# Attention laps: the query softmax's last product moved to POOL, and new orders on PE, DVE and POOL

## The chip, the cores and the metric

The kernel runs on one core of one Trainium2 chip. The metric is the device time of one execution in microseconds. TensorE is called PE here (its weight loads PEld), VectorE DVE, ScalarE ACT, GpSimd POOL, SyncE SP.

## The reference

One model layer over 8 rows of 512 tokens. The token part is a small recurrent memory, a layer norm, four feed-forward blocks of width 128 and 512, and a head to 64 values. Then comes linear attention with 4 heads of 32, and then a mixture of 8 experts with the best 2 per token. Each part is added to its own input. The change touches only the attention:

```python
xn = rmsnorm(x, g_pre)
q, k, v = split(xn @ w_qkv)              # 4 heads of 32, 4 memory columns are put before k and v
q = softmax(q, over the 32 of a head) * SCALE
k = softmax(k, over the sequence)
context = einsum('bhdn,bhen->bhde', k, v)
out = einsum('bhde,bhdn->bhen', context, q)
out = rmsnorm(out @ w_out + b_out, g_out) + x
```

## The kernel before

Everything stays in SBUF, and every engine has its own instruction list, written out by hand. Engines meet only at counting semaphores: `wait_ge(sem, n)` holds an engine's whole list until the count is reached. There are three stages: the token part (32 steps of a row and a layer, to about 248 us), the attention in nine overlapping laps (to about 318 us), and the experts (64 units of a row and an expert).

The laps are the loops `for m in range(FIRST_LAP, 0)`, one on each engine. This text counts them by a = m + 9, so lap 0 to lap 8. In lap a an engine works on several rows at once, each at another step: row a (keys, query projections), c = a - 1 (softmaxes, context), d = a - 2 (attend), e = a - 3 (output norm, residual), f = a - 4 (normalised input of the experts), and rows a + 1 to a + 3 (normalised input of the attention). k is the row's parity and picks one of two buffers.

The operations of a lap before the change, in order, with the lines of their instructions:

- PE: `k_transposes(c)` (L1675, L1676), `q_transposes(d)` (L1692, waits for `qn_ready`), `z_transposes(a+1)`, `context(c)`, `keep_clock` (three products whose result nobody reads), `projected_context(c)` (waits for `ctm_ready`), `expert_z_transposes(f)` (waits for `ezlo_ready`), `attend(d)` (waits for `m_ready`, for `qt_ready` and for `h1_ready` of row e), in lap 1 `head(7)`, `keys(a+1)` (waits for ACT's `zt_ready` and for `m_ready` of row c, whose bank it writes), `queries_and_values(a+1)`. Lap 7 has `logits(0)` at its end. Products recorded on L1430 are of several kinds, told apart by their tiles.
- DVE: `max_k(a)` (L1164), `negated` (L1168), `output_sums(e)` (L1216), `max_q(a)` (L1176), `sub_q(a)` (L1180), `softmaxes(c)` (L1190 to L1198), `z_of(a+2)` (L1092), `masked_context(c)` (L1205, waits for `ctx_done`), `expert_z_lo(f)` (L1235), `head_out` of row 5 or 6 in laps 0 and 1 (L1103), `scaled_output(e)` (L1224, waits for POOL's `r2_ready`), `z_lo(a+2)` (L1098), `scaled_m(c)` (L1210, waits for `m_done`), `residual_moments(e)` (L1074, L1077), in lap 1 `head_out(7)`, and in laps 0 to 2 `head_moments(a+5)`.
- ACT: `output_squares(e)`, `k_turned(c)`, `q_turned(d)`, `ez_of(f)` (L796, waits for POOL's `s1_ready`), `ez_hi(f)` (L802), `exp_k(a)`, `z_hi(a+2)` (L718), `z_turned(a+1)` (L756), `copy_v(a)`, `expert_z_turned(f)`, `exp_q(a)`.
- POOL: `expert_norm(f)` (L564 to L569), `centred(a+3)` (L540), `output_norm(e)` (L556, L558), `roots_of(a+3)` (L530, L531, L534), `residual_base(a+2)` (L548, L551, waits for DVE's `z_ready`). The powers in L534, L558 and L567 are inverse square roots.

PSUM has eight banks. The bank of `keys(a+1)` is the one that `context`, `projected_context` and `scaled_m` of row c use, so keys wait for `scaled_m(c)`.

Of the kernel before, what the change touches and what calls it, by code (L numbers as in the profile page):

```python
# [29 lines left out]
ALU = mybir.AluOpType  # L30
# [3 lines left out]
P = 128  # L34
B, S, V = 8, 512, 64
NT = S // P
# [3 lines left out]
HEADS, DH, NMEM = 4, 32, 4  # L40
# [112 lines left out]
def build(nc, tok_in, emb_in, wupd_in, wf_in, w1_in, w2_in, headw_in, cols_in, rows_in, cons_in,  # L153
          wqkv_in, wout_in, memv_in, wr_in, ew1_in, ew2_in, eb2_in, out_hbm):
    ctx = ExitStack()
    with ctx:
# [3 lines left out]
        def sem(name):  # L160
            return ctx.enter_context(nc.semaphore(name))
# [100 lines left out]
        q_sb = x  # L262
# [7 lines left out]
        qsum = sb("qsum", [P, 2, NT * HEADS])  # L270
        qrec = sb("qrec", [P, 2, NT * HEADS])
# [82 lines left out]
        k_done, qv_done = sem("k_done"), sem("qv_done")  # L354
        kmax_ready, kexp_ready, v_ready = sem("kmax_ready"), sem("kexp_ready"), sem("v_ready")
        qsub_ready, qexp_ready, qn_ready = sem("qsub_ready"), sem("qexp_ready"), sem("qn_ready")
        k_t, kt_ready, q_t, qt_ready = sem("k_t"), sem("kt_ready"), sem("q_t"), sem("qt_ready")
        ctx_done, ctm_ready, m_done, m_ready = (sem("ctx_done"), sem("ctm_ready"), sem("m_done"),
                                                sem("m_ready"))
# [23 lines left out]
        def row64(first):  # L383

            return rows[:, first:first + D2].unsqueeze(1).broadcast_to([P, NT, D2])

        def o_view(b):

# [60 lines left out]
        def _(pool):  # L449
# [93 lines left out]
            def residual_base(b):  # L543
# [6 lines left out]
                own.wait(v)  # L550
                pool.tensor_tensor(h0[:, b, :], h0[:, b, :], xc[:, b % 2, :], ALU.add).then_inc(res_ready, 1)  # L551

            def output_norm(b, k):

                pool.wait_ge(osum_ready, b + 1)
                v = own.inc(pool.tensor_scalar(e2o[:, k, :], osum[:, k, :], 1.0 / D2, 1e-24 / D2, ALU.mult, ALU.max))  # L556
                own.wait(v)
                pool.tensor_tensor(r2[:, k, :], e2o[:, k, :], mhalf[:, 0:NT], ALU.pow).then_inc(r2_ready, 1)  # L558

            def expert_norm(b, k):  # L560

                pool.wait_ge(mv1_ready, b + 1)
                mv, vi = mv1[:, k, :, :], h1v[:, k, :, :]
                v = own.inc(pool.tensor_scalar(vi[:, 0, :], mv[:, :, 1], 1.0 + EPS, EPS * EPS, ALU.mult, ALU.add))  # L564
                own.inc(pool.tensor_scalar(vi[:, 1, :], mv[:, :, 0], -1.0, None, ALU.mult))
                own.wait(v)
                v = own.inc(pool.tensor_tensor(s1[:, k, :], vi[:, 0, :], mhalf[:, 0:NT], ALU.pow))  # L567
                own.wait(v)
                pool.tensor_tensor(s1_shift[:, k, :], vi[:, 1, :], s1[:, k, :], ALU.mult).then_inc(s1_ready, 1)  # L569
# [4 lines left out]
                if b:  # L574
                    residual_base(b - 1)
            for m in range(FIRST_LAP, 0):
                a, e, f = m + 9, m + 6, m + 5
                if f >= 0:
                    expert_norm(f, f % 2)
                if a + 3 < B:  # L580
                    centred(a + 3)
                if e >= 0:
                    output_norm(e, e % 2)
                if a + 3 < B:
                    roots_of(a + 3)
                if a + 2 < B:
                    residual_base(a + 2)
# [306 lines left out]
        def _(dve):  # L894
# [206 lines left out]
            def head_out(b):  # L1101
                dve.wait_ge(head_done, b + 1)
                dve.tensor_tensor(tiles(h0[:, b, :]), tiles(bank[HEAD_BANK[b % 2]][:, 0:NT * D2]), row64(R_HEADB),  # L1103
                                  ALU.add).then_inc(h0_ready, 1)
# [76 lines left out]
                                  qmax[:, k, :].rearrange("p (t h) -> p t h", h=HEADS).unsqueeze(3)  # L1181
                                  .broadcast_to([P, NT, HEADS, DH]), ALU.subtract).then_inc(qsub_ready, 1)

            def q_by_head(b):
                return q_sb[:, b, :].rearrange("p (a d) -> p a d", d=DH)

            def softmaxes(b, k):

                dve.wait_ge(qexp_ready, b + 1)
                v = own.inc(dve.reduce_sum(qsum[:, k, :], q_by_head(b), AX.X))  # L1190
                v_k = own.inc(dve.tensor_scalar(kstat[:, k, 4:5], kstat[:, k, 2:3], kstat[:, k, 3:4], float(DH) ** 0.5,
                                                ALU.add, ALU.mult))
                own.wait(v)
                v = own.inc(dve.reciprocal(qrec[:, k, :], qsum[:, k, :]))
                own.wait(v_k)
                v_k = own.inc(dve.reciprocal(kstat[:, k, 5:6], kstat[:, k, 4:5]))
                own.wait(v)
                dve.tensor_tensor(q_by_head(b), q_by_head(b), qrec[:, k, :].unsqueeze(2)  # L1198
                                  .broadcast_to([P, NT * HEADS, DH]), ALU.mult).then_inc(qn_ready, 1)
                return v_k  # L1200

            def masked_context(b, k):

                dve.wait_ge(ctx_done, b + 1)
                dve.tensor_tensor(ctm[:, k, :], bank[4 * k + 1][:, P:2 * P], blkmask, ALU.mult).then_inc(ctm_ready, 1)  # L1205

            def scaled_m(b, k, v):
                own.wait(v)
                dve.wait_ge(m_done, b + 1)
                dve.scalar_tensor_tensor(mx_sb[:, b % 4, :], bank[4 * k + 1][:, 2 * P:3 * P], kstat[:, k, 5:6],  # L1210
                                         bout_share[:, :], ALU.mult, ALU.add).then_inc(m_ready, 1)
# [107 lines left out]
            for m in range(FIRST_LAP, 0):  # L1319
                a, c, e, f = m + 9, m + 8, m + 6, m + 5  # L1320
                if a < B:
                    max_k(a, a % 2)
                    negated(a % 2, own.n)
                if e >= 0:
                    output_sums(e, e % 2)
                if a < B:
                    max_q(a, a % 2)
                    sub_q(a, a % 2, own.n)
                if m == -1:
                    v = first_hot(0, v)  # L1330
                if c >= 0:
                    v_total[c] = softmaxes(c, c % 2)
                if a + 2 < B:
                    z_of(a + 2, a % 2)
                if c >= 0:
                    masked_context(c, c % 2)
                if f >= 0:
                    expert_z_lo(f, f % 2)
                if a == 0:
                    head_out(5)  # L1340
                if a == 1:
                    head_out(6)
                if e >= 0:
                    scaled_output(e, e % 2)
                if a + 2 < B:
                    z_lo(a + 2, a % 2)
                if m == -1:
                    v = second_max(0, v)
                if c >= 0:
                    scaled_m(c, c % 2, v_total[c])  # L1350
                if m == -1:
                    v = second_hot(0, v)
                if e >= 0:
                    residual_moments(e, e % 2)
                if m == -2:
                    take_logits(0)
                if m == -1:
                    v = weights(0, v)
                    gates_out(0, v)
                if m == -2:  # L1360
                    v = first_max(0)
                if a == 1:
                    head_out(7)
                if a < 3:
                    head_moments(a + 5)
# [62 lines left out]
        def _(pe):  # L1428
# [335 lines left out]
            for m in range(FIRST_LAP, 0):  # L1764
                a, c, d, f = m + 9, m + 8, m + 7, m + 5
                if c >= 0:
                    k_transposes(c, c % 2)
                if d == 0:
                    pe.wait_ge(h0_ready, B)
                if d >= 0:  # L1770
                    q_transposes(d, d % 2)
                if a + 1 < B:
                    z_transposes(a + 1, (a + 1) % 2)
                if c >= 0:
                    context(c, c % 2)
                keep_clock(c)
                if c >= 0:
                    projected_context(c, c % 2)
                if f >= 0:
                    expert_z_transposes(f, f % 2)  # L1780
                if d >= 0:
                    attend(d, d % 2)
                if m == -1:
                    keep_clock(c)
                if a == 1:
                    head(7)
                if a + 1 < B:
                    keys(a + 1, (a + 1) % 2)
                if a == 0:
                    head(5)  # L1790
                if m == -1:
                    pe.wait_ge(late_weights, 4)
                    pe.wait_ge(m_ready, B)
                    hidden(0)
                    hidden(1)
                    turn_gates(0)
                if a + 1 < B:
                    queries_and_values(a + 1, (a + 1) % 2)
                if m == -2:
                    logits(0)  # L1800
                if a == 0:
                    head(6)
# [132 lines left out]
```

## Time and profile before

| what | value |
|---|---|
| median of 3 runs | 423.93 us (423.75 to 424.1) |
| the profiled execution | 424.18 us |
| its span in the trace | 422.4 us |
| mean granted clock of PE | 0.982 |
| instructions | 6309 |

The span is the time from the first to the last instruction; 1.8 us lie around it. The page tells each engine's busy time and the chain of work that ended last. The timelines give every instruction's start and duration; where several instructions of a line stand together, the row gives their number. Durations overlap a little: the next operation of an engine can start before the one in front of it is recorded as ended, so the step from start to start is what an operation costs its engine. What stands in square brackets is the idle time in front of the operation and who ended it.

### The profile page before, as it was taken

How to read it: one execution, taken by the hardware profiler on the slowest of the kernel's cores; microseconds unless marked ns; L12 is line 12 of the kernel's file. 1: busy time of each engine (PE TensorE's matmuls, PEld its weight loads, DVE VectorE, ACT ScalarE, POOL GpSimd, SP SyncE). 2: the span in 40 equal slices, each digit the busy share in tenths (PEclk: the TensorE clock that was granted, in tenths of full speed). 3: DMA queues.
4: the chain of work that ended last, by engine and by line, in shares of the span. 5: the costliest groups of instructions: out<-in, count | busy, mean ns of one | idle time of the engine just before them, and what ended most of it. 6: DMA issues, size and time to landing. Idle time of an engine off the chain costs nothing.

```text
span 422.4 us, 6309 instructions
## 1 busy us (share of the span) xinstructions
PE 394.1 (93%) x1989; PEld 318.0 (75%) x1989; DVE 352.6 (83%) x851; ACT 326.1 (77%) x558; POOL 262.2 (62%) x388
## 2 busy tenths in 40 slices
PE   5798889999999999999999989999987998999995
PEld 2586578888888888888888878787766775876883
DVE  4887688888898889888889888999875888899885
ACT  1263689999999999888977854678846898988994
POOL 0575787778777779778776556685322654435452
PEclk9999999999999999999999998999996998999999
DMA  6800012122312321221112000000000000000001
GB/s 217 334 2 0 2 26 46 31 51 51 50 27 50 51 53 27 50 50 50 44 32 51 1 0 2 2 2 2 0 2 0 0 2 12 15 12 12 14 13 26
DMA packets 15849, 14.94 MB, mean 35 GB/s; under 512 B 9796, under 2 KB 10568, under 8 KB 15560
## 3 DMA queue, kind: packets, MB, share of 16 engines
q1 hardware_dynamic: 15816, 14.54, 13.8%
q8 instruction: 16, 0.26, 0.2%
q14 instruction: 17, 0.14, 0.1%
HBM read 13.42 MB, written 1.11 MB: 34 GB/s over the span
## 4 chain that ended last, share of the span: by engine, by line
PE 64%; DVE 18%; ACT 12%; issue 4%; DMA 1%; POOL 1%; SPq 0%; DVEq 0%; ACTq 0%
PE ps L1430 56%; PE ps L1453 4%; ACT hid L861 4%; ACT w_all L867 3%; ACT ezf L796 2%; DVE hid L1372 2%; DVE hh L1224 2%; DVE stats L941 1%; DVE x L1372 1%; PE ps L1461 1%; DVE st L1074 1%; DVE kstat L1164 1%; DMA xn<-in_w_f 1%; DVE xn_lo L1379 1%; DVE qmax L1176 1%
## 5 line engine op out<-in xcount | busy, mean ns | idle before, releaser
L675 ACT ACTIVATE hid<-ps,b_fold 128x512 f32<-128x512 f32 x128 | 84.0, 681 | 21.3 <-PE ps L1430 20.8
L1015 DVE TENSOR_TENSOR hid_lo<-hid,hid_hi 128x1024 fp32r<-128x1024 f32 x64 | 78.8, 1231 | 25.3 <-ACT hid_hi L680 25.1
L1430 PE MATMUL ps<-xn_hi,w_all 128*128 128x512 f32 x256 | 87.4, 402 | 0.6 <-DVE xn_lo L1010 0.6
L1430 PE MATMUL ps<-hid_hi,w_all 128*128 128x512 f32 x256 | 85.0, 393 | 0.0
L680 ACT ACTIVATE hid_hi<-hid 128x1024 fp32r<-128x1024 f32 x64 | 67.9, 1061 | 2.0
L1430 PEld LDWEIGHTS ps<-xn_hi,w_all 128*128 128x128 f32 x256 | 48.4, 189 | 10.8 <-issue 0.9
L1430 PEld LDWEIGHTS ps<-hid_hi,w_all 128*128 128x128 f32 x256 | 48.1, 188 | 9.9
L1430 PE MATMUL ps<-xn_lo,w_all 128*128 128x512 f32 x128 | 49.9, 390 | 0.0
L1430 PE MATMUL ps<-hid_lo,w_all 128*128 128x512 f32 x128 | 49.8, 389 | 0.0
L861 ACT ACTIVATE hid<-ps,eb_fold 128x512 f32<-128x512 f32 x64 | 44.1, 689 | 1.4 <-PE ps L1430 1.2
L1430 PE MATMUL ps<-hid_hi,ew 128*128 128x512 f32 x128 | 43.1, 421 | 1.9 <-ACT hid L861 1.8
L1372 DVE TENSOR_TENSOR hid<-hid,ps 128x512 f32<-128x512 f32 x44 | 30.0, 683 | 11.2 <-ACT hid L861 7.7
L941 DVE BATCH_NORM_STATS2 stats<-ps 128x6 f32<-128x128 f32 x160 | 35.2, 282 | 2.8 <-PE ps L1453 2.8
L490 POOL TENSOR_TENSOR var_in<-var_in 128x4 f32<-128x4 f32 x30 | 35.7, 1191 | 2.4
L486 POOL TENSOR_TENSOR var_in<-stats 128x4 f32<-128x4 f32 x30 | 17.6, 586 | 25.6 <-DVE stats L941 25.6
L1430 PE MATMUL ps<-w_all,ew 128*128 128x512 f32 x84 | 31.6, 415 | 1.2 <-DVE xn_lo L1379 0.7
L494 POOL TENSOR_TENSOR var_in<-var_in,mhalf 128x4 f32<-128x4 f32 x30 | 31.1, 1036 | 2.3
L1453 PEld LDWEIGHTS ps<-cons,x 128*128 128x128 f32 x160 | 23.2, 187 | 10.9 <-issue 5.3
L867 ACT ACTIVATE w_all<-hid 128x512 fp32r<-128x512 f32 x44 | 28.0, 636 | 4.3 <-DVE hid L1372 4.2
L1430 PEld LDWEIGHTS ps<-hid_hi,ew 128*128 128x128 f32 x128 | 23.8, 197 | 9.4 <-ACT hid L861 4.8
L1453 PE MATMUL ps<-cons,x 128*128 128x128 f32 x160 | 25.5, 281 | 5.3 <-DVE stats L941 2.9
L1430 PE MATMUL ps<-hid_lo,sel 128*128 128x512 f32 x64 | 27.2, 424 | 1.8 <-ACT hid_lo L817 0.8
(222 smaller groups left out, 898.2 us busy)
## 6 DMA issues: line engine op xcount, KB each, us to landing
rstd_row<-roots SPq DMA_DIRECT2D x29, 256.0 KB, 3.8
hh<-in_tokens SPq DMA_DIRECT2D x8, 256.0 KB, 7.9
hid<-in_w SPq DMA_DIRECT2D x1, 1024.0 KB, 7.1
rstd_row<-in_w SPq DMA_DIRECT2D x1, 1024.0 KB, 10.2
out<-hh SPq DMA_DIRECT2D x7, 128.0 KB, 2.0
ew_raw<-in_expert_w SPq DMA_DIRECT2D x1, 512.0 KB, 9.7
roots<-rstd SPq DMA_DIRECT2D x29, 2.0 KB, 1.4
ew_raw<-in_expert_w SPq DMA_DIRECT2D x1, 256.0 KB, 9.9
```

Source lines behind the costliest of these rows:

```text
L486: own.inc(pool.tensor_tensor(vi[:, 0, :], st[:, :, 1], st[:, :, 4], ALU.subtract))
L490: own.inc(pool.tensor_tensor(vi[:, 0, :], vi[:, 0, :], vi[:, 0, :], ALU.mult))
L494: v = own.inc(pool.tensor_tensor(vi[:, 0, :], vi[:, 2, :], mhalf[:, 0:NT], ALU.pow))
L675: act.activation(hid[:, j % 2, f, :], bank[f], ACT.Gelu, bias=b1_fold[:, j // B * F + f:j // B * F + f + 1]).then_inc(gelu_done, 1)
L680: act.activation(hid_hi[:, j % 2, 2 * p:2 * p + 2, :], hid[:, j % 2, 2 * p:2 * p + 2, :], ACT.Copy).then_inc(hhi_ready, 1)
L861: act.activation(hg[:, n % NHG, :], bank[HIDDEN_BANK[n % 2]], ACT.Gelu, bias=eb1_fold[:, n % E:n % E + 1]).then_inc(eg_done, 1)
L867: act.activation(hw_hi[:, slot * S:(slot + 1) * S], hw(slot), ACT.Copy).then_inc(hwhi_act, 1)
L941: last = dve.bn_stats(stats6[:, slot, t, :], bank[TB][:, t * P:(t + 1) * P])
L1015: dve.tensor_tensor(hid_lo[:, j % 2, 2 * p:2 * p + 2, :], hid[:, j % 2, 2 * p:2 * p + 2, :], hid_hi[:, j % 2, 2 * p:2 * p + 2, :].bitcast( ...
L1372: dve.tensor_tensor(hw(slot), hg[:, n % NHG, :], bank[spread_bank(n)], ALU.mult).then_inc(hw_ready, 1)
L1430: return pe.matmul(out, lhsT, rhs, start=start, stop=stop)
L1453: last = pe.transpose(bank[TB][:, t * P:(t + 1) * P], part, ident)
```

## The change

Four edits in the laps:

1. DVE's product of q's exponentials with the reciprocals of their sums (L1198) goes. POOL does it in a new `softmax_of_queries(c)`, which waits for the new semaphore `qrec_ready`.
2. POOL's lap becomes `expert_norm(f)`, `output_norm(e)`, `softmax_of_queries(c)`, `centred(a+3)`, `roots_of(a+3)`, `residual_base(a+2)`.
3. On DVE `masked_context(c)` comes before `z_of(a+2)`, and `scaled_m(c)` before `scaled_output(e)`.
4. On PE `keys(a+1)` comes before `attend(d)`, and so in lap 1 before `head(7)`.

```diff
--- before.py
+++ after.py
@@ -354,6 +354,7 @@
         k_done, qv_done = sem("k_done"), sem("qv_done")
         kmax_ready, kexp_ready, v_ready = sem("kmax_ready"), sem("kexp_ready"), sem("v_ready")
         qsub_ready, qexp_ready, qn_ready = sem("qsub_ready"), sem("qexp_ready"), sem("qn_ready")
+        qrec_ready = sem("qrec_ready")
         k_t, kt_ready, q_t, qt_ready = sem("k_t"), sem("kt_ready"), sem("q_t"), sem("qt_ready")
         ctx_done, ctm_ready, m_done, m_ready = (sem("ctx_done"), sem("ctm_ready"), sem("m_done"),
                                                 sem("m_ready"))
@@ -383,6 +384,9 @@
         def row64(first):
 
             return rows[:, first:first + D2].unsqueeze(1).broadcast_to([P, NT, D2])
+
+        def q_by_head(b):
+            return q_sb[:, b, :].rearrange("p (a d) -> p a d", d=DH)
 
         def o_view(b):
 
@@ -550,6 +554,12 @@
                 own.wait(v)
                 pool.tensor_tensor(h0[:, b, :], h0[:, b, :], xc[:, b % 2, :], ALU.add).then_inc(res_ready, 1)
 
+            def softmax_of_queries(b, k):
+
+                pool.wait_ge(qrec_ready, b + 1)
+                pool.tensor_tensor(q_by_head(b), q_by_head(b), qrec[:, k, :].unsqueeze(2)
+                                   .broadcast_to([P, NT * HEADS, DH]), ALU.mult).then_inc(qn_ready, 1)
+
             def output_norm(b, k):
 
                 pool.wait_ge(osum_ready, b + 1)
@@ -574,14 +584,15 @@
                 if b:
                     residual_base(b - 1)
             for m in range(FIRST_LAP, 0):
-                a, e, f = m + 9, m + 6, m + 5
+                a, c, e, f = m + 9, m + 8, m + 6, m + 5
                 if f >= 0:
                     expert_norm(f, f % 2)
+                if e >= 0:
+                    output_norm(e, e % 2)
+                if c >= 0:
+                    softmax_of_queries(c, c % 2)
                 if a + 3 < B:
                     centred(a + 3)
-                if e >= 0:
-                    output_norm(e, e % 2)
-                if a + 3 < B:
                     roots_of(a + 3)
                 if a + 2 < B:
                     residual_base(a + 2)
@@ -1181,9 +1192,6 @@
                                   qmax[:, k, :].rearrange("p (t h) -> p t h", h=HEADS).unsqueeze(3)
                                   .broadcast_to([P, NT, HEADS, DH]), ALU.subtract).then_inc(qsub_ready, 1)
 
-            def q_by_head(b):
-                return q_sb[:, b, :].rearrange("p (a d) -> p a d", d=DH)
-
             def softmaxes(b, k):
 
                 dve.wait_ge(qexp_ready, b + 1)
@@ -1191,13 +1199,9 @@
                 v_k = own.inc(dve.tensor_scalar(kstat[:, k, 4:5], kstat[:, k, 2:3], kstat[:, k, 3:4], float(DH) ** 0.5,
                                                 ALU.add, ALU.mult))
                 own.wait(v)
-                v = own.inc(dve.reciprocal(qrec[:, k, :], qsum[:, k, :]))
+                dve.reciprocal(qrec[:, k, :], qsum[:, k, :]).then_inc(qrec_ready, 1)
                 own.wait(v_k)
-                v_k = own.inc(dve.reciprocal(kstat[:, k, 5:6], kstat[:, k, 4:5]))
-                own.wait(v)
-                dve.tensor_tensor(q_by_head(b), q_by_head(b), qrec[:, k, :].unsqueeze(2)
-                                  .broadcast_to([P, NT * HEADS, DH]), ALU.mult).then_inc(qn_ready, 1)
-                return v_k
+                return own.inc(dve.reciprocal(kstat[:, k, 5:6], kstat[:, k, 4:5]))
 
             def masked_context(b, k):
 
@@ -1330,24 +1334,24 @@
                     v = first_hot(0, v)
                 if c >= 0:
                     v_total[c] = softmaxes(c, c % 2)
+                if c >= 0:
+                    masked_context(c, c % 2)
                 if a + 2 < B:
                     z_of(a + 2, a % 2)
-                if c >= 0:
-                    masked_context(c, c % 2)
                 if f >= 0:
                     expert_z_lo(f, f % 2)
                 if a == 0:
                     head_out(5)
                 if a == 1:
                     head_out(6)
+                if c >= 0:
+                    scaled_m(c, c % 2, v_total[c])
                 if e >= 0:
                     scaled_output(e, e % 2)
                 if a + 2 < B:
                     z_lo(a + 2, a % 2)
                 if m == -1:
                     v = second_max(0, v)
-                if c >= 0:
-                    scaled_m(c, c % 2, v_total[c])
                 if m == -1:
                     v = second_hot(0, v)
                 if e >= 0:
@@ -1778,14 +1782,14 @@
                     projected_context(c, c % 2)
                 if f >= 0:
                     expert_z_transposes(f, f % 2)
+                if a + 1 < B:
+                    keys(a + 1, (a + 1) % 2)
                 if d >= 0:
                     attend(d, d % 2)
                 if m == -1:
                     keep_clock(c)
                 if a == 1:
                     head(7)
-                if a + 1 < B:
-                    keys(a + 1, (a + 1) % 2)
                 if a == 0:
                     head(5)
                 if m == -1:
```

## Rows read from the trace of the kernel before

**Rows 1.** The page's first part: each engine's busy time, share of the span and instructions.
```profile
PE 394.1 (93%) x1989; PEld 318.0 (75%) x1989; DVE 352.6 (83%) x851; ACT 326.1 (77%) x558; POOL 262.2 (62%) x388
```

**Rows 2.** The chain that ended last, in order of time, lap 5: start, us, what.
```profile
289.45 2.67 PE ps L1430 x18
```

**Rows 3.** The timeline of PE in lap 1: start us, us, what, count.
```profile
259.66 0.38 PE L1430 MATMUL ps<-wout,scratch 128*128 128x128 f32 x2
259.88 1.00 PE L1430 MATMUL ps<-headw,x 128*128 128x64 f32 x8
```

**Rows 4.** The timeline of DVE, laps 1 to 6, the same columns.
```profile
260.92 0.42 DVE L1103 TENSOR_TENSOR hh<-ps,rows 128x256 f32<-128x256 f32 x1 [0.38 <-PE ps L1430]
...
265.05 0.25 DVE L1194 RECIPROCAL qrec<-qsum 128x16 f32<-128x16 f32 x1
...
272.69 0.42 DVE L1092 TENSOR_TENSOR scratch<-scratch,sr 128x256 f32<-128x256 f32 x1
...
286.97 0.69 DVE L1198 TENSOR_TENSOR x<-x,qrec 128x512 f32<-128x512 f32 x1
...
289.24 0.85 DVE L1098 TENSOR_TENSOR w_all<-scratch,w_all 128x256 fp32r<-128x256 f32 x1
...
296.07 0.85 DVE L1224 SCALAR_TENSOR_TENSOR hh<-ps,r,hh 128x64 f32<-128x64 f32 x4
```

**Rows 5.** The timeline of POOL, laps 2 to 5.
```profile
266.53 0.61 POOL L548 TENSOR_TENSOR scratch<-scratch,sr 128x256 f32<-128x256 f32 x1 [4.26 <-DVE scratch L1092]
...
268.09 0.62 POOL L540 TENSOR_TENSOR scratch<-hh,mv 128x256 f32<-128x256 f32 x1
269.93 0.26 POOL L556 TENSOR_SCALAR e2o<-osum 128x4 f32<-128x4 f32 x1 [1.22 <-DVE osum L1216]
...
271.28 0.23 POOL L530 TENSOR_SCALAR sr_in<-mv 128x4 f32<-128x4 f32 x1
...
271.75 1.67 POOL L534 TENSOR_TENSOR sr<-sr_in,mhalf 128x8 f32<-128x8 f32 x1
...
283.94 0.19 POOL L564 TENSOR_SCALAR h1v<-mv 128x4 f32<-128x4 f32 x1
...
285.81 0.23 POOL L556 TENSOR_SCALAR e2o<-osum 128x4 f32<-128x4 f32 x1
...
289.08 0.72 POOL L551 TENSOR_TENSOR hh<-hh,scratch 128x256 f32<-128x256 f32 x1
```

**Rows 6.** POOL's groups by shape: count, then busy us and mean ns of one.
```profile
L593 POOL TENSOR_TENSOR xn_lo<-hid,w_all 128x512 fp32r<-128x512 f32 x10 | 13.0, 1296 | 15.7 <-ACT w_all L867 15.7
```

**Rows 7.** The timeline of ACT in lap 5.
```profile
286.08 1.42 ACT L796 ACTIVATE ezf<-hh,s_shift,s 128x64 f32<-128x64 f32 x4
...
289.10 0.58 ACT L756 ACTIVATE xn_hi<-ps 128x512 fp32r<-128x512 f32 x1
```

**Rows 8.** The timeline of PE, laps 5 to 7.
```profile
297.07 1.13 PE L1430 MATMUL ps<-mx_sb,qT 128*128 128x128 f32 x8 [0.21 <-DVE hh L1224]
297.95 0.70 PE L1430 MATMUL ps<-xn_hi,wqkv 128*128 128x512 f32 x2
298.50 1.08 PE L1430 MATMUL ps<-wqkv,xn_hi 128*128 128x256 f32 x8
299.41 0.60 PE L1675 MATMUL ps<-cons,scratch 128*128 128x128 f32 x4
...
303.26 0.38 PE L1430 MATMUL ps<-wout,scratch 128*128 128x128 f32 x2
...
304.53 1.13 PE L1430 MATMUL ps<-mx_sb,qT 128*128 128x128 f32 x8 [0.21 <-DVE hh L1224]
```

**Rows 9.** PE in two-microsecond windows: stretch, us, busy, granted clock, DMA.
```profile
254.00:256.00 2.00, 2.00 (x11) 0.50 0.03 8
```

**Rows 10.** The timeline of PE where that clock was low.
```profile
252.70 1.18 PE L1430 MATMUL ps<-wqkv,xn_hi 128*128 128x256 f32 x8 [1.51 <-ACT rstd_row L773]
...
255.24 1.06 PE L1675 MATMUL ps<-cons,scratch 128*128 128x128 f32 x4
```

## The prediction

> **What bounds the kernel now.** The page's first part comes first: PE is busy 93% of the span, DVE 83%, ACT 77%, POOL 62% [rows 1]. That is an average, and the change touches only the nine attention laps (about 249 to 318 us), so the rest was read from the timelines of those laps, engine by engine, and from the chain in order of time. In the laps PE and DVE are both nearly full. DVE goes from the maximum of the keys to `scaled_output`, that lets `attend` start on PE, `attend` with the next keys and projections holds PE for 2.67 us in the chain [rows 2], and the keys let DVE begin its next lap. From lap 4 on the chain also runs through ACT's `ez_of`. One attend to the next takes 7.46 us in lap 6 (297.07 to 304.53) and 7.62 in lap 5 (289.45 to 297.07) [rows 2, 8]. POOL looks idle for a third of the time, but its order matters: each of its waits is a place where it is ahead. I write op(b) for an operation on row b, and all times of "after" below are worked out by walking the four engine queues from lap 1, each operation starting at the later of its engine and its waits.
>
> **The change part by part.**
>
> *The multiply leaves DVE.* Per row one 0.69 us operation goes at 286.97 [rows 4], about 0.61 from start to start. This is a gain on DVE only where DVE doesn't wait. After the change `masked_context` comes directly behind the reciprocals and needs the context from PE, whose loop doesn't get shorter, so most of the 0.61 turns into a wait there. I count it as nothing in the sum; its full worth stands in the first rival.
>
> *The multiply comes to POOL.* The nearest row is POOL's 128x512 product of the expert stage, 1.30 us [rows 6]; two of its 128x256 operations would be 1.22 (0.61 each) [rows 5]. I take 1.29. What is queued behind it counts more than its length: it waits for the reciprocals of its row, in the middle of DVE's lap, and `centred`, `roots_of` and `residual_base` of the lap, which used to run ahead, stand behind that wait. The pieces, start to start [rows 5]: output norm 1.35 (269.93 to 271.28), roots 2.14 (271.28 to 271.75 plus 1.67), residual 1.56 (266.53 to 268.09), centred 0.62, expert norm 1.87 (283.94 to 285.81). Lap 2 then asks 1.29+0.62+2.14+1.56 = 5.6 us of POOL, lap 3 with the output norm 7.0, lap 4 with the expert norm too 8.8, which is more than a lap is long. Together 21.4 us, without a wait in between.
>
> *The shared way to SBUF.* DVE's `z_lo` reads two SBUF tensors. While POOL's addition ran (289.08, 0.72) it took 0.85 us (289.24) [rows 4, 5], though such an operation takes 0.42 when undisturbed at 272.69 [rows 4]. POOL's multiply will meet `z_of` or `expert_z_lo` in every lap; the one that waited goes first when it ends, and then holds up `centred` by some 0.3. Three laps of this and one more for the roots: 1.2 us on POOL's queue. The low end is 0, if they never meet.
>
> The Trainium skill ("SBUF — State Buffer", Who interferes with whom) says that a Vector instruction with two SBUF inputs and a GpSimd instruction that reads SBUF exclude each other for the whole instruction. For streaming operations this trace agrees (0.85 against 0.42). For the power it does not: `z_of` at 272.69 took its plain 0.42 while POOL's 1.67 us power was running [rows 4, 5]. By the rule taken word for word every power would shut DVE out as well, before and after alike; by the rows only the new multiply does. It changes no term above.
>
> *Keys before attend on PE, and head 7 behind the keys (lap 1).* Keys(2) need `scaled_m(0)`, which needs the product that PE starts at 259.66 [rows 3]: 0.42 to its end, 0.49 for `scaled_m` (0.34 and the hand-over, an estimate by the 0.42 us rows), so keys(2) start about 260.6, hardly earlier than before. Head 7 used to fill this gap at 259.88 [rows 3]; now it starts after the 0.55 us keys (297.95 to 298.50 in lap 6) [rows 8], at 261.15, which is 1.27 later. DVE's `head_out(7)` (260.92 before) [rows 4] and all that follows it, so the whole of lap 2, come 1.27 later.
>
> *What that makes of POOL.* The reciprocals of row 1 come at 265.05 [rows 4] + 1.27, and 0.30 later, at 266.6, POOL starts its multiply. It then has work without a pause: 266.6 + 21.4 + 1.2 = 289.2 for the start of expert norm(1), which ran at 283.94 [rows 5]. So POOL, not DVE, sets laps 4 and 5. s1(1) follows 1.87 later at 291.1; ACT's `ez_of(1)` ran at 286.08 [rows 7].
>
> *What hangs on it.* ACT reaches the copy of z(6) 3.02 us behind that (286.08 to 289.10) [rows 7], at 294.1, and 0.6 on the keys(6) can start, 294.7. Here the new PE order costs: attend(3) stands behind these keys and starts 0.55 later, at 295.3, against 289.45 [rows 2]. From attend to the transposes of the next lap it was 2.34 (297.07 to 299.41) [rows 8] with the keys in it, 1.79 without. So they come at 297.1 instead of 289.45 + 2.5 (a small wait included) = 292.0. **Plus 5.1 us at the start of lap 6.**
>
> *Laps 6 to 8.* POOL has caught up. Now `scaled_m` lies between the projected context and `scaled_output`, so the loop is: attend 0.88, projections 0.91, transposes to projected context 3.85 (299.41 to 303.26), 0.42, `scaled_m` 0.27, `scaled_output` to attend 1.00 (296.07 to 297.07) [rows 4, 8] = 7.33, against 7.46. In lap 6 POOL's multiply holds `expert_z_lo` for 0.3, so it is 0.2 longer; in lap 7 there are no keys to take out of the loop, and only `scaled_m` 0.27 comes in: 0.3. Lap 8 waits for the expert rows before and after and gives nothing back, although DVE is 0.6 less loaded. Together 0.5.
>
> *The clock.* With POOL late, PE stands 1.8 to 2.2 us in front of the keys in laps 2, 4 and 5. After the 1.51 us idle before 252.70 the granted clock fell to 0.50 (1.2 GHz) in the stretch 254 to 256, and four transposes took 1.06 us instead of 0.60; waits of 0.2 us did nothing [rows 8 to 10]. In laps 2 and 4 a fall is hidden, because POOL sets what comes next. In lap 6 it is not: projections and transposes there would be some 0.8 longer. Between 0 and 1.3 I take 0.8, as our wait is nearer to the 1.51.
>
> **The sum:** 5.1 + 0.5 + 0.8 = 6.4 us. The expert stage behind it is unchanged and starts with the gates that lap 8 makes, so it moves as a whole. The profiled execution took 424.18 (its span 422.4 and 1.8 around it): 430.6. The median of the runs, 423.93, is 0.25 below that execution, so 430.3.
>
> **The rivals.**
> 1. *The cover holds* (faster). POOL's own idle time takes the multiply, and the keys never wait for ACT's copy. Then DVE has 0.61 less, and PE's own work is the floor: lap 6's 7.46 less the 0.21 idle before its attend [rows 8], 7.25. Three laps of 7.6 (lap 5 is one of them) and lap 6 come down to that: 3 x 0.37 + 0.21 = 1.3 us saved, 422.6. It decides at the place where expert norm(1) starts: at 284 or earlier it holds. Against it speaks the sum of POOL's lap 4, 8.8 us. 7%.
> 2. *POOL hardly binds, the orders do.* If the multiply costs POOL next to nothing, head 7's 1.27 and the keys ahead of attend still remain, since z(6) comes from ACT 0.6 before the keys: by the same walk 2.7 us, 426.6. For it: spans on POOL are rough. 14%.
> 3. *No collisions and no lower clock.* 5.1 + 0.5 - 1.3 = 4.3: 428.2. This is the low part of the forecast's own case.
> 4. *The clock falls in more laps, or the multiply with its broadcast operand takes 1.5 us.* 0.2 more in each of six multiplies is 1.2, and a second exposed fall 0.8: 432.3. 13%.
> 5. *Nothing changes*, DVE's gain and POOL's delay balancing: 3%.
>
> **How the numbers follow.** The forecast with its low part (3.) has 63%: 427.8 to 431.6. To leave out no more than 2 in 10 the range reaches down to the second rival and up through the fourth: 426.3 to 433.0. About 0.2% is what a measurement of this kernel can tell from no change: faster 0.07, within it 0.03, slower 0.90.
>
> **What would show it.** In the profile after: POOL without a pause from about 266.6 to 295, its multiplies 1.3 us each; expert norm(1) near 289 (at 284 the main term is wrong); `head_out(7)` near 262.2 (at 260.9 the first step is wrong); `z_of` or `expert_z_lo` of 0.8 to 1.4 us instead of 0.42; PE idle about 2 us before keys(5) and keys(6), with ACT's copy of z as releaser; attends at about 269.7, 277.2, 286, 295.3; a granted clock of 0.50 somewhere in laps 2 to 6 or none; laps 6 and 7 a little longer than before. If POOL is idle within laps 3 and 4, or DVE waits for nothing, the walk is wrong from its start.

## The result: 1.4% slower

The changed kernel takes 429.35 us, the median of 4 runs (427.87 to 429.83); the kernel before took 424.01 beside it. The ratio is 1.0136, with a 95% interval of 1.0109 to 1.0163, so about 5.3 to 5.8 us more. The profiled execution is the fastest of the four: 427.87, with a span of 426.1.

The first part of the page after, to be read against [rows 1]:

```profile
PE 391.4 (92%) x1989; PEld 314.9 (74%) x1989; DVE 349.3 (82%) x843; ACT 326.5 (77%) x558; POOL 270.2 (63%) x396
```

POOL is busy 8 us more (eight multiplies of 1.05), DVE 3.3 less. The averages say nothing of a loss; the order of the work does. The lines of the changed kernel are shifted by some: its multiply is L560, expert norm L574 to L579, roots L538, `z_of` L1103, `expert_z_lo` L1239, `masked_context` L1209, `head_out` L1114. The timeline of POOL in laps 2 to 5, as [rows 5] of before:

```profile
265.59 1.05 POOL L560 TENSOR_TENSOR x<-x,qrec 128x512 f32<-128x512 f32 x1 [3.66 <-DVE qrec L1202]
...
272.88 1.05 POOL L560 TENSOR_TENSOR x<-x,qrec 128x512 f32<-128x512 f32 x1 [0.42 <-DVE qrec L1202]
...
278.26 0.19 POOL L574 TENSOR_SCALAR h1v<-mv 128x4 f32<-128x4 f32 x1
...
281.47 1.05 POOL L560 TENSOR_TENSOR x<-x,qrec 128x512 f32<-128x512 f32 x1
...
283.71 1.97 POOL L538 TENSOR_TENSOR sr<-sr_in,mhalf 128x8 f32<-128x8 f32 x1
...
287.15 0.19 POOL L574 TENSOR_SCALAR h1v<-mv 128x4 f32<-128x4 f32 x1
...
288.74 0.20 POOL L579 TENSOR_TENSOR s_shift<-h1v,s 128x4 f32<-128x4 f32 x1
```

In front of the first multiply shown POOL waited 3.66 us for the reciprocals. Of the operations after it only one has an idle time: 0.42 before the multiply of lap 3. Otherwise POOL works without a pause to 292.95 and reaches expert norm(1) at 287.15; it was 283.94. The chain in order of time shows what hangs on it:

```profile
265.73 1.20 DVE scratch L1103
...
267.90 2.58 PE ps L1434 x18
270.50 0.70 DVE qmax L1187
...
272.88 1.05 POOL x L560
...
288.74 0.21 POOL s_shift L579
...
288.97 1.44 ACT ezf L807 x4
...
292.11 0.49 ACT xn_hi L767
...
292.64 2.56 PE ps L1434 x18
```

From 272.88 to 288.95 every piece of the chain is POOL's: a 16 us stretch in which no other engine sets the pace. Before the change POOL stood nowhere in the chain of the laps. From `s_shift` the chain goes to ACT's `ez_of(1)` (288.97, 2.89 later than in [rows 7]), on to the copy of z(6) (292.11) and to PE's keys, attend and projections.

The timeline of PE in laps 1 and 5:

```profile
258.31 0.38 PE L1434 MATMUL ps<-wout,scratch 128*128 128x128 f32 x2
259.53 0.73 PE L1434 MATMUL ps<-xn_hi,wqkv 128*128 128x512 f32 x2 [0.83 <-ACT xn_hi L767]
260.09 1.00 PE L1434 MATMUL ps<-headw,x 128*128 128x64 f32 x8
...
292.64 0.74 PE L1434 MATMUL ps<-xn_hi,wqkv 128*128 128x512 f32 x2 [0.26 <-ACT xn_hi L767]
293.22 1.05 PE L1434 MATMUL ps<-mx_sb,qT 128*128 128x128 f32 x8
...
295.04 0.60 PE L1679 MATMUL ps<-cons,scratch 128*128 128x128 f32 x4
```

In lap 1 PE stands idle for 0.83 us before the keys, and only then comes head 7 (x8 on headw). In lap 5 the keys start at 292.64, the attend behind them at 293.22; before, the attend ran at 289.45 [rows 2]. The timeline of DVE:

```profile
261.13 0.42 DVE L1114 TENSOR_TENSOR hh<-ps,rows 128x256 f32<-128x256 f32 x1 [1.64 <-PE ps L1434]
...
265.65 1.27 DVE L1103 TENSOR_TENSOR scratch<-scratch,sr 128x256 f32<-128x256 f32 x1
...
281.17 0.41 DVE L1103 TENSOR_TENSOR scratch<-scratch,sr 128x256 f32<-128x256 f32 x1
282.01 0.79 DVE L1239 TENSOR_TENSOR ew_raw<-ezf,ew_raw 128x256 fp32r<-128x256 f32 x1 [0.43 <-ACT ew_raw L813]
...
289.30 0.29 DVE L1209 TENSOR_TENSOR scratch<-ps,cons 128x128 f32<-128x128 f32 x1 [0.62 <-PE ps L1434]
```

`z_of(4)` (265.65) takes 1.27 us instead of 0.42 and `expert_z_lo(0)` (282.01) 0.79, each beside one of POOL's multiplies; `z_of(6)` (281.17), a little ahead of one, takes its plain 0.41. The stretched `z_of(4)` stands in the chain (265.73, 1.20): through ACT it holds up PE's keys at 267.90. So in lap 2 the multiply delays the loop by a collision, before POOL's queue does so from lap 3 on. At 289.30 `masked_context` had waited for the context: there went most of the 0.61 us that DVE was spared.

**A base that can be compared.** The profiled executions differ by 3.7 us only, the medians by 5.3. Most of this is the clock: the profiled execution of before had its granted clock at 0.50 from about 254 to 257 [rows 9], the one of after has 1.00 up to 323. (Both have further stretches at 0.50 behind the gates; from there to the end they need 104.0 and 103.8 us.) So from here on the schedules are compared by a distance inside one execution: from the first transposes of row 0's keys (lap 1) to the end of the gates, with which lap 8 ends. The "falls" in the table are stretches of about 3.4 us at a clock of 0.50 that lie in this distance; the one of before lies at its start, and a second begins only as its gates end. Each ratio is to the kernel before as timed beside that run on its chip (medians of 422.6 to 424.0). The ratios and intervals are of fast executions alone, while the median and the spread of dve_only include its one slow one, 429.83.

| kernel | median, us | ratio to before, 95% | distance, us | falls in it |
|---|---|---|---|---|
| before | 424.01 | | 63.2 | 1 |
| before_fill | 422.79 | 0.9995 (0.9975 to 1.0015) | 62.7 | 0 |
| after | 429.35 | 1.0136 (1.0109 to 1.0163) | 67.8 | 0 |
| after_fill | 430.07 | 1.0181 (1.0143 to 1.0219) | 67.8 | 1, in lap 8 |
| mult_back | 427.14 | 1.0092 (1.0071 to 1.0112) | 66.0 | 0 |
| pool_only | 426.05 | 1.0078 (1.0055 to 1.0100) | 66.0 | 2 |
| pe_only | 429.70 | 1.0158 (1.0134 to 1.0181) | 68.5 | 1 |
| dve_only | 426.32 | 1.0068 (1.0037 to 1.0099) | 65.6 | 1 |
| narrow_fill | 426.86 | 1.0085 (1.0057 to 1.0112) | 65.4 | 1 |
| double_fill | 433.95 | 1.0266 (1.0232 to 1.0300) | 72.5 | 3 |
| head_first_fill | 428.92 | 1.0140 (1.0083 to 1.0196) | 66.6 | 1 |
| keys_last_fill | 427.83 | 1.0119 (1.0069 to 1.0170) | 68.0 | 2 |
| mult_last_fill | 427.69 | 1.0107 (1.0058 to 1.0157) | 65.6 | 0 |
| shared_fill | 421.63 | 0.9962 (0.9933 to 0.9991) | 62.5 | 1 |

After against the filled kernel before, both free of falls: 67.8 - 62.7 = 5.1 us.

### The profile page after: what moved, and what is told of

Read it like the earlier page. It is cut to its first block, busy times and chain, and to the rows that moved or that the text cites. A ratio compares the mean times of both kernels' runs of the same rounds, so it can differ in the third digit from the quotient of the medians.

```text
span 426.1 us, 6309 instructions
## 1 busy us (share of the span) xinstructions
PE 391.4 (92%) x1989; PEld 314.9 (74%) x1989; DVE 349.3 (82%) x843; ACT 326.5 (77%) x558; POOL 270.2 (63%) x396
## 3 DMA queue, kind: packets, MB, share of 16 engines
HBM read 13.42 MB, written 1.11 MB: 34 GB/s over the span
## 4 chain that ended last, share of the span: by engine, by line
PE 62%; DVE 15%; ACT 14%; POOL 4%; issue 3%; DMA 1%; SPq 0%; POOLq 0%; DVEq 0%; ACTq 0%
PE ps L1434 55%; PE ps L1457 4%; ACT hid L872 4%; ACT w_all L878 4%; ACT ezf L807 2%; DVE hid L1376 2%; DVE stats L952 1%; DVE x L1376 1%; PE ps L1465 1%; POOL sr L538 1%; DVE hh L1228 1%; DMA xn<-in_w_f 1%; DVE xn_lo L1383 1%; DVE st L1085 1%; ACT scratch L868 1%
## 5 line engine op out<-in xcount | busy, mean ns | idle before, releaser
L1434 PE MATMUL ps<-hid_hi,ew 128*128 128x512 f32 x128 | 42.1, 412 | 2.0 <-ACT hid L872 1.8
```

The costliest lines, as they stand in the source:

```text
L1434: return pe.matmul(out, lhsT, rhs, start=start, stop=stop)
```

## The experiments

The first four take the change apart. "Theory A" in the expectations is the walk of the prediction with the multiply at 1.03 us from start to start.

**mult_back**: the new orders without the move.

```diff
-                if c >= 0:
-                    softmax_of_queries(c, c % 2)
...
+                dve.tensor_tensor(q_by_head(b), q_by_head(b), qrec[:, k, :].unsqueeze(2)
+                                  .broadcast_to([P, NT * HEADS, DH]), ALU.mult).then_inc(qn_ready, 1)
```

> The changed kernel with the multiply back on DVE (the new orders on PE and DVE stay). Theory A (the walk: POOL's queue and the new orders each cost, and the orders alone are not free, since head 7 and attend stand behind the keys): 2.9 us above the kernel before, 426.9. Theory B (the multiply on POOL is the whole cause, the orders cost nothing): 424.0, no difference from before.

Measured: 427.14, ratio 1.0092; distance 66.0, 3.3 above the filled kernel before. Theory B falls: two thirds of the loss are there with the multiply still on DVE. POOL does not stand in its chain of laps 2 to 5. The move adds 1.8 to it (67.8 - 66.0).

**pool_only**: the move and POOL's order without the new orders of PE and DVE.

```diff
-                if a + 1 < B:
-                    keys(a + 1, (a + 1) % 2)
                 if d >= 0:
                     attend(d, d % 2)
...
+                if a + 1 < B:
+                    keys(a + 1, (a + 1) % 2)
```

(DVE's two places are put back in the same way.)

> The kernel before with the multiply on POOL and POOL's new order alone; PE and DVE keep the old order. Theory A: 3.0 us above before, 427.0, expert norm(1) again late on POOL. Theory B: all of the loss, 429.4. Theory C (the orders are the cause, POOL has room): 423 to 424.

Measured: 426.05, ratio 1.0078, which is 3.3 us; distance 66.0, with two falls in it. Between A and B, nearer to A. Expert norm(1) is late on POOL again, as A has it, and POOL works without a pause from the multiply of lap 2 (265.28) up to there:

```profile
286.20 0.19 POOL L574 TENSOR_SCALAR h1v<-mv 128x4 f32<-128x4 f32 x1
```

So the move costs 3.3 us on top of the old orders and 1.8 on top of the new ones: its price depends on what stands beside it.

**pe_only** and **dve_only**: one order alone on the kernel before.

```diff
+                if a + 1 < B:
+                    keys(a + 1, (a + 1) % 2)
                 if d >= 0:
                     attend(d, d % 2)
```

> The kernel before with PE's new order alone (keys before attend and before head 7). Theory A: scaled_m still comes at the end of DVE's lap, so the keys wait for it and attend waits behind them: 4.2 us above before, 428.2. Theory B: 424.0.

Measured: 429.70, ratio 1.0158, which is 6.7 us where Theory A said 4.2; distance 68.5 with a fall in lap 2. PE's new order by itself costs about as much as the whole change (the intervals overlap). Its keys wait for a `scaled_m` that DVE still does late, behind `scaled_output`, and attend waits behind them. DVE, then PE, in lap 3:

```profile
275.54 0.85 DVE L1224 SCALAR_TENSOR_TENSOR hh<-ps,r,hh 128x64 f32<-128x64 f32 x4
...
276.64 0.35 DVE L1210 SCALAR_TENSOR_TENSOR mx_sb<-ps,kstat,bout_share 128x128 f32<-128x128 f32 x1
...
277.14 0.70 PE L1430 MATMUL ps<-xn_hi,wqkv 128*128 128x512 f32 x2 [0.94 <-DVE mx_sb L1210]
```

The same wait for `scaled_m` (L1210) stands in laps 1 to 6, 0.46 to 1.11 us long.

```diff
                 if c >= 0:
                     masked_context(c, c % 2)
                 if a + 2 < B:
                     z_of(a + 2, a % 2)
...
+                if c >= 0:
+                    scaled_m(c, c % 2, v_total[c])
                 if e >= 0:
                     scaled_output(e, e % 2)
```

> The kernel before with DVE's new order alone (masked_context before z_of, scaled_m before scaled_output). Theory A: z_of stands behind the context and scaled_output behind the projected context: 1.8 us above before, 425.8. Theory B: 424.0.

Measured: 426.32, ratio 1.0068, with a wide spread (423.16 to 429.83); distance 65.6, and of before with its fall 63.2, so 2.4 more; Theory A said 1.8. By the ratios the three parts alone add up to 3.0% and the whole is 1.4%; the two orders cost 1.6% and 0.7% alone and 0.9% together (mult_back). They offset each other in part.

**before_fill** and **after_fill**: the clock taken out of the comparison.

```diff
+                if a == 0:
+                    fill(2 * REPEATS, bank[0])
...
                     hidden(1)
+                    fill(2 * REPEATS, bank[3])
                     turn_gates(0)
+                    fill(REPEATS, bank[3])
```

> The kernel before with idle stretches of PE filled by products that nobody reads: six 128x512 products in lap 0 before the projections of row 1, six before the gates are turned and three behind that. Theory A (the clock falls to 0.50 after such idle stretches and costs 1.3 us at 254 and some 1 to 2 us at 318): the granted clock stays at 1.00 through the laps, 421 to 422.5, with less spread. Rival (the low clock costs nothing on the path): no difference, or slower by up to 2 us where a filler runs into work.

Measured: 422.79, ratio 0.9995, interval 0.9975 to 1.0015: no gain in the median. But the profiled execution, 421.0, kept the full clock throughout. The table of PE by stretches (busy, then granted clock), its first and its last line before the experts are under way:

```profile
248.00:256.00 8.00, 7.52 (x50) 1.00 0.01 2
...
312.00:320.00 8.00, 7.14 (x39) 1.00 0.00 1
```

Against the profile of before it reached the first transposes 0.9 us earlier, of which it already led by 0.2 in front of the fall, and it needed 0.5 less for the distance, so the fall at 254 costs about 1.2 us. Of its twelve runs, the two with a mean clock of 1.000 took 421.0 and 421.2, those at 0.986 about 424.5. The fillers do not keep the clock up in every run.

> The changed kernel with the same three fillers. Theory A: what the change costs is the schedule and not the clock, so it stays 4.8 to 5.3 us above the filled kernel before. Rival (the changed kernel loses by falls of the clock in its longer idle stretches): the distance shrinks to under 4.

Measured: 430.07, ratio 1.0181, and the distance is 67.8 as without fillers. The difference to the filled kernel before does not shrink. The loss is the schedule. Its one fall cost nothing: lap 8 took 11.36 us with it and 11.36 in the changed kernel without.

**narrow_fill** and **double_fill**: POOL's multiply cut to 32 columns, and doubled.

```diff
-                pool.tensor_tensor(q_by_head(b), q_by_head(b), qrec[:, k, :].unsqueeze(2)
-                                   .broadcast_to([P, NT * HEADS, DH]), ALU.mult).then_inc(qn_ready, 1)
+                pool.tensor_tensor(q_by_head(b)[:, 0:1, :], q_by_head(b)[:, 0:1, :], qrec[:, k, 0:1].unsqueeze(2)
+                                   .broadcast_to([P, 1, DH]), ALU.mult).then_inc(qn_ready, 1)
```

> The filled changed kernel where POOL multiplies only the first 32 of 512 columns (the other exponentials stay without their divisor, so the output is not the reference's). Theory A (POOL's queue sets laps 3 to 5): the walk gives 2.0 us less than the filled changed kernel, and 2.8 above the filled kernel before, which is what the new orders cost by themselves. Theory B (POOL alone): level with the filled kernel before. Theory C (POOL has room): no difference from the filled changed kernel.

Measured: 426.86; distance 65.4, 2.4 less than the filled changed kernel and 2.7 above the filled kernel before. The timeline of POOL:

```profile
265.46 0.24 POOL L560 TENSOR_TENSOR x<-x,qrec 128x32 f32<-128x32 f32 x1 [4.19 <-DVE qrec L1202]
...
276.63 0.19 POOL L574 TENSOR_SCALAR h1v<-mv 128x4 f32<-128x4 f32 x1
...
284.55 0.19 POOL L574 TENSOR_SCALAR h1v<-mv 128x4 f32<-128x4 f32 x1
...
291.60 0.19 POOL L574 TENSOR_SCALAR h1v<-mv 128x4 f32<-128x4 f32 x1 [1.34 <-DVE mv L1088]
```

The multiply is 0.24 long, and expert norm(1) comes at 284.55 instead of 287.39 in the filled changed kernel. POOL still has hardly a pause in laps 3 and 4, but it stands nowhere in the chain of laps 2 to 5: full, it no longer sets the pace. What is left over the filled kernel before is what the orders cost. Of the 2.4 us that the full multiply adds, 0.8 come in lap 2 (8.38 us in the filled changed kernel, 7.59 here), where it stretches `z_of(4)`, and 1.4 in laps 4 and 5, where POOL's queue binds.

```diff
+                v = own.inc(pool.tensor_tensor(q_by_head(b), q_by_head(b), qrec[:, k, :].unsqueeze(2)
+                                               .broadcast_to([P, NT * HEADS, DH]), ALU.mult))
+                own.wait(v)
```

> The filled changed kernel with POOL's multiply done twice in each row (the output is not the reference's). Theory A: POOL's queue is the bound in laps 2 to 5 and each microsecond on it comes out at the end: by the walk 6.0 us more than the filled changed kernel. Theory C (POOL has room): under 1 us more.

Measured: 433.95, 3.9 above the filled changed kernel by the medians, 4.7 by the distance. The timeline of POOL:

```profile
274.84 1.05 POOL L560 TENSOR_TENSOR x<-x,qrec 128x512 f32<-128x512 f32 x1
275.97 1.11 POOL L563 TENSOR_TENSOR x<-x,qrec 128x512 f32<-128x512 f32 x1
...
291.37 0.19 POOL L577 TENSOR_SCALAR h1v<-mv 128x4 f32<-128x4 f32 x1
```

Counted from the first transposes, expert norm(1) moved from 32.7 us (filled changed kernel) to 36.4 (291.37 - 254.98). Of these 3.7 us, 0.6 lie before POOL's first multiply of lap 2, where this execution has a fall of the clock; the other 3.1 are about what three extra multiplies make, 1.12 each from start to start, less the pause of 0.4 that is gone. With less and with more work POOL's queue shows as the bound. Why 4.7 came where 6.0 was expected is left open, and the 4.7 still holds three falls.

**head_first_fill**, **keys_last_fill** and **mult_last_fill**: one place in a queue each.

```diff
+                if a == 1:
+                    head(7)
                 if a + 1 < B:
                     keys(a + 1, (a + 1) % 2)
                 if d >= 0:
                     attend(d, d % 2)
```

> The filled changed kernel with head(7) ahead of the keys in lap 1, as before the change. Theory A (head 7 behind the keys delays lap 2 and with it POOL's queue): gates 1.3 us earlier than in the filled changed kernel (322.5), 1.3 us less in all. Rival (POOL's queue alone decides, lap 1's delay is swallowed): no difference.

Measured: 428.92, ratio 1.0140; distance 66.6, 1.2 less than the 67.8 of the filled changed kernel. Up to the start of lap 8, and so without its fall, which stretched that lap by 0.3, it is 1.55 less. This execution was late by 1.6 us already before the laps (its clock fell once at 31 us, as in mult_last_fill, which was late by as much), so the gates' time of day, 322.9, says nothing, and the distance does. `head_out(7)` on DVE:

```profile
261.38 0.42 DVE L1114 TENSOR_TENSOR hh<-ps,rows 128x256 f32<-128x256 f32 x1
```

That is 5.1 us after the first transposes (256.26); in the changed kernel it was 6.7 (261.13 - 254.46).

```diff
                 if d >= 0:
                     attend(d, d % 2)
...
+                if a + 1 < B:
+                    keys(a + 1, (a + 1) % 2)
```

> The filled changed kernel with attend ahead of the keys again (and head 7 ahead of them). Theory A: 0.5 us less than the filled changed kernel only, as the keys then come later for DVE while POOL's queue still binds; gates at about 322.0. Rival (keys before attend is most of the loss): 3 us or more less.

Measured: 427.83, ratio 1.0119; distance 68.0, but with two falls, one of them in lap 5, which took 10.5 us instead of 8.9. Up to the start of lap 5 it is 1.8 ahead of the filled changed kernel, but head_first_fill is 1.5 ahead there, so putting attend first adds only 0.2. Lap 6 then takes 7.96 us instead of 7.61, as PE waits 0.69 before attend for a `scaled_output` that stands behind `scaled_m`. By the ratios it is faster than the filled changed kernel by 0.6%, with intervals that overlap. The rival's 3 is not reached; what attend and keys cost by themselves stays open, and no more than a few tenths show up to lap 5.

```diff
-                if c >= 0:
-                    softmax_of_queries(c, c % 2)
                 if a + 3 < B:
                     centred(a + 3)
                     roots_of(a + 3)
                 if a + 2 < B:
                     residual_base(a + 2)
+                if c >= 0:
+                    softmax_of_queries(c, c % 2)
```

> The filled changed kernel with POOL's multiply at the end of its lap, behind residual_base, so that centred, roots_of and residual_base no longer stand behind the wait for the reciprocals. Theory A (the place in POOL's queue costs, not the multiply's length alone): 1.8 us less, gates at 320.7. Rival (only the amount of work on POOL counts): no difference.

Measured: 427.69, ratio 1.0107; distance 65.6, 2.2 less. The amount of work is the same, so its place costs about 2 of the 5 us. With its place mended the multiply on POOL costs next to nothing: 65.6, where it is 65.4 with the narrow one and 66.0 with it on DVE (mult_back). The timeline of POOL in lap 5:

```profile
286.75 0.19 POOL L574 TENSOR_SCALAR h1v<-mv 128x4 f32<-128x4 f32 x1
...
291.87 1.04 POOL L560 TENSOR_TENSOR x<-x,qrec 128x512 f32<-128x512 f32 x1
```

The multiply of row 4 now stands last, at 291.87. Expert norm(1) is at 30.4 us after the first transposes (256.32) here and 32.7 in the changed kernel (287.15 - 254.46).

**shared_fill**: the kernel before with fillers, and a multiply on POOL only where it has room, at the end of its lap.

```diff
+                if c >= 0 and c not in (2, 3):
+                    softmax_of_queries(c, c % 2)
...
+                if b in (2, 3):
+                    dve.wait_ge(qrec_ready, b + 1)
+                    dve.wait_ge(qn_ready, b)
+                    dve.tensor_tensor(q_by_head(b), q_by_head(b), qrec[:, k, :].unsqueeze(2)
+                                      .broadcast_to([P, NT * HEADS, DH]), ALU.mult).then_inc(qn_ready, 1)
```

> A version that should beat both: the orders of the kernel before on PE, DVE and POOL, with fillers; POOL multiplies at the end of its lap for rows 0, 1 and 4 to 7, where it has room, and DVE for rows 2 and 3. Theory A: 0.6 us less than the filled kernel before, gates at 316.4, 422.2. Rival (collisions on SBUF and the later qn take it back): level or up to 1 us more.

Measured: 421.63, ratio 0.9962, interval 0.9933 to 0.9991: faster than the kernel before on its chip, by 1.6 us (1.3 by the medians). Its distance of 62.5 holds a fall inside lap 8. PE there:

```profile
305.50 0.87 PE L1687 MATMUL ps<-cons,scratch 128*128 128x128 f32 x4
...
306.44 1.09 PE L1704 MATMUL ps<-cons,x 128*128 128x128 f32 x4
```

The transposes of the keys took 0.87 and those of q 1.09 us instead of 0.60. Up to that point it was 0.5 ahead of the filled kernel before (50.95 against 51.42 us from the first transposes). Whether it also beats that kernel in the median is not settled: 0.9962 and 0.9995 were measured on different chips, and their intervals touch. POOL's multiplies in laps 2, 6 and 7:

```profile
266.06 1.05 POOL L561 TENSOR_TENSOR x<-x,qrec 128x512 f32<-128x512 f32 x1
...
293.07 1.05 POOL L561 TENSOR_TENSOR x<-x,qrec 128x512 f32<-128x512 f32 x1 [0.21 <-DVE qrec L1204]
...
300.54 1.05 POOL L561 TENSOR_TENSOR x<-x,qrec 128x512 f32<-128x512 f32 x1 [0.85 <-DVE qrec L1204]
```

## Why the prediction was right, step by step

The forecast was 430.3 and the range 426.3 to 433.0. The sum of 5.6 us for the schedule measured 5.1, and the 0.8 us for the clock did not belong where the step put it. That the median, 429.35, came within 1 us of the forecast is in part luck: the three other runs of the changed kernel took 1.1 to 2.0 us more than the profiled one, at mean clocks of 0.984 to 0.988 instead of 0.995, and no trace shows where. Lap by lap the distance grew by 1.1, 1.2, 0.2, 0.7, 1.1, 0.2, 0.5 and 0.1 us in laps 1 to 8. Counted from the first transposes of row 0 and against the filled kernel before (0.12 us taken off for its earlier start):

- **Head 7 behind the keys.** 1.27 were forecast; `head_out(7)` came 1.55 later, and putting head 7 back in front gave 1.55 back up to lap 8. The forecast was read off [rows 3], a stretch that the low clock had slowed in the kernel before: head 7 starts there 4.6 us after the first transposes, and 4.1 in the filled kernel before. The releaser of keys(2) was ACT's copy of z, not `scaled_m` as the step had it; both were due at about the same time.
- **POOL without a pause.** From the multiply of lap 2 to expert norm(1) 22.6 us were forecast, and it was 21.56 (265.59 to 287.15). The mis-sized term is the multiply: 1.05 and not 1.29 (1.0 from start to start), so 0.8 less in three; the step also had 0.4 too much of collisions, and a pause of 0.42 that it did not foresee works the other way. The row that the 1.29 came from, [rows 6], is a difference, not a product as the step has it. Expert norm(1) was 4.6 us later, where the step said 5.3.
- **Attend behind the keys.** attend(3) came 5.1 later (forecast 5.85), lap 6 began 4.4 later (forecast 5.1). In both 0.7 is what POOL's step had too much.
- **Laps 6 to 8.** 0.5 were forecast: laps 6 and 7 took 0.6 more, lap 8 0.1.
- **Collisions.** They came in every lap from 2 to 5 and stretched `z_of` or `expert_z_lo` by 0.1 to 0.9 us. POOL's `centred` took 0.80 instead of 0.62 three times and its power once 1.97 instead of 1.67, 0.8 us in all against the 1.2 of the step. The step counted them on POOL's queue only; in lap 2 the collision sits on the way from `z_of(4)` to the keys, and lap 2 grew by 1.2.
- **DVE's 0.61 counted at nothing.** It went into waits of 0.56 to 0.62 for the context in laps 3 to 7.
- **The clock.** This step failed. PE idled for 1.63 us before the keys of lap 2, and for 1.35 and 0.26 around those of lap 5, and the granted clock stayed at 1.00. Even the 1.5 us gap in lap 0, which stands in six profiles, was followed by a fall in three (before, pool_only, dve_only) and by none in three (after, mult_back, pe_only). The fall that [rows 9] show cost the kernel before about 1.2 us in its profiled execution; the term was read off a single execution.

The first rival, that the cover holds, fell with expert norm(1) at 287. The second, POOL cheap and the orders alone, is what narrow_fill is: 2.7 us, just as it was priced.

## What to carry to other kernels

An operation moved to an idle engine takes the place of everything behind it in that engine's list. So ask what it waits for, and put it behind what could run ahead. An idle share of a third was no room: from lap 3 on POOL had 6.8 us of work and then 8.9, in laps that had lasted 7.3 to 7.6, and there one more multiply with an early wait cost 2.4 us (narrow_fill) of the 5.1; at the end of POOL's lap it cost 0.2. When several lists are reordered together, time each order alone as well: here PE's new order alone costs as much as the whole change, DVE's takes part of that back, and the two together still cost 3 us.

## What the runs showed of the hardware

- POOL's product of a 128x512 tensor in place with a broadcast 128x16 took 1.05 us, and 1.11 to 1.29 in a few cases; its 128x512 difference into another type takes 1.30 [rows 6]. With the 0.24 us of the 128x32 product in narrow_fill this makes an estimated 1.7 ns per column over a fixed 0.19 us, which gives 0.62 for 256 columns, as POOL's 128x256 product took (0.61).
- A collision shows as a long duration of the operation that comes second: `z_of(4)`, started 0.06 us after POOL's multiply, took 1.27 and ended 0.28 after it. With POOL's power only the power is stretched: it took 1.97 instead of 1.67 (283.71) when DVE's `z_lo` started 0.04 us behind it, while that `z_lo` took its plain 0.41 (283.75).
- The clock falls in stretches of about 3.4 us at 0.50 (twice that long at 318 in before and at 323 in pe_only), at places that differ from one execution to the next: at 31 us in two of them; in the laps at 254, 262, 268, 281, 286, 291, 305, 311 and 314 in others, with PE busy or idle in front; at 318 to 324 in eight of the fourteen profiles and between 353 and 365 in nine. In the eight profiles whose 1.5 us gap in lap 0 is filled, no fall follows there. What sets them off is open.
- What a fall costs depends on what it meets: about 1.6 us at 31 us (the first transposes come at 256.3 instead of 254.3 to 255.0 in the filled kernels), about 1.2 at 254, 0.3 in lap 8 of head_first_fill, and nothing in lap 8 of after_fill and narrow_fill. The fastest and the slowest run of dve_only are 6.7 us apart, at mean clocks of 1.000 and 0.971.
